# A second buffer for the transposed incidence, another order in the middle of each graph, and the output's scaling on GpSimd and ScalarE

## What is computed

```python
def hypergraph_conv(x, adj, W, b):
    H = (adj != 0).astype(x.dtype)
    w = adj.reshape(N, -1)[:, :C]
    xw = einsum('ncd,hd->nch', x, W)
    Dn = einsum('nce,ne->nc', H, w);  Dn = where(Dn > 0, 1/Dn, 0)
    Be = H.sum(axis=1);               Be = where(Be > 0, 1/Be, 0)
    m = Be[:, :, None] * einsum('nce,nch->neh', H, xw)
    return Dn[:, :, None] * einsum('nce,neh->nch', H, m) + b

def gnn(x):                       # 256 -> 512 -> 256
    h = layer_norm(relu(hypergraph_conv(x, adj, W1, b1)), gamma, beta)
    return hypergraph_conv(h, adj, W2, b2) + x

def ffn(x):
    topw, topi = top_k(x @ router_w + router_b, 2);  topw = softmax(topw)
    h = silu(einsum('td,edh->teh', x, expert_w) + expert_b)
    y = x + einsum('te,teh->th', mask(topi, topw), h) @ out_w + out_b
    return norm_w * (y / sqrt(mean(y * y) + 1e-6))

x = x + gnn(_layernorm(x))
x = x + ffn(_layernorm(x))
```

## Time and profile before

| what | us |
|---|---|
| median of 3 runs | 750.67 |
| lowest and highest | 749.53, 751.47 |
| the profiled execution, its time | 751.47 |
| the profiled execution, its span | 749.9 |
| TensorE busy | 705.3 |
| VectorE busy | 652.2 |
| ScalarE busy | 495.0 |
| GpSimd busy | 288.4 |

### The profile page before, as it was taken

How to read it: one execution, slowest core, us unless ns; L and a number is a source line. 1 busy time by engine, 2 the same in 40 slices (tenths; PEclk the granted TensorE clock), 3 DMA queues, 4 the chain that set the end, 5 groups by cost and what they waited for, 6 DMA issues and landing times.

```text
span 749.9 us, 16620 instructions
## 1 busy us (share of the span) xinstructions
PE 705.3 (94%) x5573; PEld 482.4 (64%) x5573; DVE 652.2 (87%) x1569; ACT 495.0 (66%) x971; POOL 288.4 (38%) x670
## 2 busy tenths in 40 slices
PE   4787999999999999999999999999999999999983
PEld 3364584766758486675858577584857768585671
DVE  4878888889898989989898899988899998988776
ACT  4655757667594856758585766858576685847562
POOL 4223334144353525444351434435153453524242
PEclk9988999999999999999999999999999999999997
DMA  8455538376583838657393765738385664727312
GB/s 290 169 110 201 113 89 239 67 225 131 162 178 94 240 64 229 135 172 164 90 245 60 237 122 182 154 105 231 62 247 111 202 134 129 184 64 184 58 29 56
DMA packets 42584, 111.65 MB, mean 149 GB/s; under 512 B 4160, under 2 KB 5312, under 8 KB 42560
## 3 DMA queue, kind: packets, MB, share of 16 engines
q0 software_dynamic: 13536, 41.42, 30.4%
q1 hardware_dynamic: 29024, 69.92, 28.3%
HBM read 69.91 MB, written 16.25 MB: 115 GB/s over the span
## 4 chain that ended last, share of the span: by engine, by line
DVE 29%; PE 26%; DMA 14%; ACT 13%; issue 12%; POOL 2%; SPq 2%; DVEq 0%; POOLq 0%; ACTq 0%
DMA xb<-xn 13%; PE bank L1261 5%; DVE comb L863 4%; PE bank L1263 4%; PE bank L1262 4%; PE bank L1346 4%; PE bank L1347 4%; DVE silu L859 4%; DVE hntl L878 3%; DVE z L867 3%; DVE ybn L980 2%; DVE x L974 2%; DVE h L741 2%; DVE ht L745 2%; ACT xsh L449 2%
## 5 line engine op out<-in xcount | busy, mean ns | idle before, releaser
L1261 PE MATMUL bank<-xth,ewh 128*128 128x512 f16 (+1 forms) x272 | 100.6, 370 | 2.1 <-DVE ewl L782 2.1
L1263 PE MATMUL bank<-xth,ewl 128*128 128x512 f16 (+1 forms) x272 | 100.7, 370 | 0.0
L1262 PE MATMUL bank<-xtl,ewh 128*128 128x512 f16 (+1 forms) x272 | 100.7, 370 | 0.0
L507 ACT ACTIVATE silu<-bank,ebcol,ksc 128x512 f32<-128x512 f32 x120 | 92.1, 769 | 7.3 <-PE bank L1263 7.2
L1261 PE MATMUL bank<-w2h,hnth 128*128 128x256 f16 x256 | 70.7, 276 | 3.3 <-DVE hntl L878 2.6
L1263 PE MATMUL bank<-w2h,hntl 128*128 128x256 f16 x256 | 70.5, 275 | 0.0
L1262 PE MATMUL bank<-w2l,hnth 128*128 128x256 f16 x256 | 70.5, 275 | 0.0
L548 ACT ACTIVATE a1h<-bank,be 128x256 f16<-128x256 f32 x64 | 26.8, 469 | 54.3 <-PE bank L1406 51.0
L654 ACT ACTIVATE uh<-bank,be 128x256 f16<-128x256 f32 x64 | 26.8, 470 | 53.4 <-PE bank L1347 53.4
L525 ACT ACTIVATE hnth<-bank 128x512 f16<-128x512 f32 x64 | 37.9, 592 | 33.3 <-PE bank L1315 33.3
L1405 PE MATMUL bank<-xsh,h 128*128 128x256 f16 x256 | 58.3, 277 | 0.9 <-DVE xsl L764 0.9
(11 more groups left out here) (248 smaller groups left out, 2138.3 us busy)
## 6 DMA issues: line engine op xcount, KB each, us to landing
adjin<-adj SPq DMA_DIRECT2D x16, 1024.0 KB, 5.3
adjtin<-adjt SPq DMA_DIRECT2D x16, 1024.0 KB, 6.2
xin<-x SPq DMA_DIRECT2D x16, 512.0 KB, 4.2
xb<-xn SPq DMA_DIRECT2D x16, 512.0 KB, 8.5
xb<-x POOLq DMA_DIRECT2D x16, 512.0 KB, 8.7
xb<-b POOLq DMA_DIRECT2D x16, 512.0 KB, 5.4
xb<-vadd POOLq DMA_DIRECT2D x16, 512.0 KB, 4.5
out<-x SPq DMA_DIRECT2D x15, 512.0 KB, 6.8
```

The costliest lines, as they stand in the source:

```text
L507: af(silu[:, i % 4, :], bank[E_BANK[i]][:, :], ACT.Silu, bias=ebcol[:, i:i + 1], scale=ksc[:, 2:3]).then_inc(silu_dn, 1)
L1261: mm(outp, lh, rh, start=first, stop=False)
L1262: mm(outp, lh, rl, start=False, stop=False)
L1263: return mm(outp, ll, rh, start=False, stop=last)
```

## The change

- **Two buffers.** `ht16` becomes a pair, one for even and one for odd graphs; the loop's body is written twice (six rounds of two graphs). `prep_ht(g)` moves from the start of body g to the end of body g - 1, between the first half of y and the remainder of U.
- **SyncE.** xb<-xn goes ahead of out<-x1 and of adjtin<-adjt, so it waits for x1 of graph f and for no incidence.
- **The output's scaling.** `finish` goes from VectorE's bodies (it stays in the tail). GpSimd multiplies y by the norm weights (`weigh_y`, two instructions of 128x512, ahead of `roots_y`), and ScalarE multiplies the result by the roots (`scale_y`, four of 128x256) as the first work of the next body. VectorE's `y_part(f, 0)` also waits until the y before has been weighed and squared.
- **The first sum of the experts** goes to GpSimd (`add_half`, 128x1024, behind the hidden tiles' roots). The last sum is split in two halves, and each half of the high part of `comb` waits for its own half.
- **ScalarE's middle.** Expert 1 and tanh stand ahead of `prep_x`; `mask_copy` stands ahead of `prep_x_hi`.
- **TensorE and VectorE.** The router's first two tiles wait for the first half of xtl alone; the last transposes of the hidden tile stand ahead of the second V tile; `hnt_part(g, 3)` stands ahead of the last sum, and `ct_part(f, 0)` ahead of `v_part(g, 0)`.

```diff
-        ht16 = sb("ht16", [P, CT, C], F16)
+        ht16 = (sb("ht16_even", [P, CT, C], F16), sb("ht16_odd", [P, CT, C], F16))
...
+            with eng.Fori(3, N - 2, 2) as g:
+                body(eng, g, 1, conv=True, ffn=True, late=True, prep=True)
+                body(eng, g + 1, 0, conv=True, ffn=True, late=True, prep=True)
...
+                if ffn:
+                    f = g - 1
+                    sp.wait_ge(x1_dn, 4 * f + 4)
+                if conv:
+                    if not prep:
+                        sp.wait_ge(xn_dn, 4 * g + 4)
+                    sp.dma_start(xb[:, :, :], xn[:, :, :]).then_inc(xn_kept, 16)
+                if ffn:
+                    sp.dma_start(out[f], x1[:, :, :]).then_inc(x1_st, 16)
+                if prep:
                     sp.wait_ge(ht_made, g + 1)
                     sp.dma_start(adjtin[:, :, :], adjt[g + 1].rearrange("(t p) c -> p t c", p=P)).then_inc(adjt_in, 16)
...
+            def weigh_y(f, j, again):
+                s = slice(CG * j, CG * j + CG)
+                gp.wait_ge(y_dn, 2 * f + j + 1)
+                if j == 0 and again:
+                    gp.wait_ge(out_st, 32 * f)
+                tt(yf[:, s, :], y[:, s, :], nwb[:, :].unsqueeze(1).to_broadcast([P, CG, D]), ALU.mult).then_inc(yw_dn, 1)
...
+            def add_half(f):
+                gp.wait_ge(comb_st, 7 * f + 2)
+                tt(comb[:, :, :], comb[:, :, :], silu[:, 2:4, :], ALU.add).then_inc(half_sum, 1)
...
+            def scale_y(act, q):
+                act.wait_ge(yw_dn, 2 * q + 2)
+                act.wait_ge(rr_st, 2 * q + 2)
+                for t in range(CT):
+                    af(yf[:, t, :], yf[:, t, :], ACT.Copy, scale=yrr[:, t:t + 1]).then_inc(yf_dn, 1)
...
             def combine_sum(f, e):
-                dve.wait_ge(comb_st, 7 * f + 2 * e)
-                TT(comb[:, :, :], comb[:, :, :], silu[:, 2 * (e % 2):2 * (e % 2) + 2, :], ALU.add).then_inc(comb_st, 1)
+                if e == 2:
+                    dve.wait_ge(half_sum, f + 1)
+                dve.wait_ge(comb_st, 7 * f + 2 * e - 1)
+                for s in ((slice(0, C),) if e == 2 else (slice(0, C // 2), slice(C // 2, C))):
+                    TT(comb[:, :, s], comb[:, :, s], silu[:, 2 * (e % 2):2 * (e % 2) + 2, s], ALU.add).then_inc(comb_st, 1)
...
                 if ffn and prep:
+                    if late:
+                        dve.wait_ge(yw_dn, 2 * f)
+                        dve.wait_ge(sq_dn, 4 * f)
                     y_part(f, 0)
+                if prep:
+                    prep_ht(g + 1, 1 - odd)
...
-                    pe.wait_ge(xt_lo, 2 * f + 2)
                     for t in range(CT):
+                        if t % CG == 0:
+                            pe.wait_ge(xt_lo, 2 * f + t // CG + 1)
```

More of the change, by code:

```diff
@@ L53, in build @@
     CG = 2
-    assert (C, D, DH, NE) == (512, 256, 512, 4)
+    assert (C, D, DH, NE) == (512, 256, 512, 4) and N % 2 == 0
     with ExitStack() as ctx:
@@ L221, in steps @@
         def steps(eng, body, tail):
[L223 to L228, removed]
+            body(eng, 0, 0, conv=True, ffn=False, late=False, prep=True)
+            body(eng, 1, 1, conv=True, ffn=True, late=False, prep=True)
+            body(eng, 2, 0, conv=True, ffn=True, late=True, prep=True)
+            with eng.Fori(3, N - 2, 2) as g:
+                body(eng, g, 1, conv=True, ffn=True, late=True, prep=True)
+                body(eng, g + 1, 0, conv=True, ffn=True, late=True, prep=True)
+            body(eng, N - 1, 1, conv=True, ffn=True, late=True, prep=False)
             tail(eng)
@@ L254, in _, with body @@
                 sp.dma_start(dst, src).then_inc(c_in, 16)
-            def body(sp, g, conv, ffn, late, prep):
+            def body(sp, g, odd, conv, ffn, late, prep):
                 if prep:
@@ L405, in body @@
                 if ffn and prep:
+                    weigh_y(f, 0, late)
+                    weigh_y(f, 1, late)
                     roots_y(f, ALL, 0)
@@ L556, in x2_part, with body @@
                        scale=yrs[:, t:t + 1]).then_inc(x2_dn, 1)
-            def body(act, g, conv, ffn, late, prep):
-                f = g - 1
+            def body(act, g, odd, conv, ffn, late, prep):
+                f, q = g - 1, g - 2
+                if late:
+                    scale_y(act, q)
                 if conv:
@@ L588, in body @@
                     expert(act, f, 0)
+                if ffn:
+                    expert(act, f, 1)
+                    act.wait_ge(arg_dn, f + 1)
+                    af(th[:, :, :], arg[:, :, :], ACT.Tanh).then_inc(th_dn, 1)
                 if prep and ffn:
                     prep_x(g + 1, (0, 1))
-                if ffn:
-                    act.wait_ge(arg_dn, f + 1)
-                    af(th[:, :, :], arg[:, :, :], ACT.Tanh).then_inc(th_dn, 1)
-                    expert(act, f, 1)
                 if prep and ffn:
@@ L992, in degrees, with body @@
                 v.reciprocal(be[:, :], dmax[:, :]).then_inc(be_dn, 1)
-            def body(dve, g, conv, ffn, late, prep):
+            def body(dve, g, odd, conv, ffn, late, prep):
                 f, q = g - 1, g - 2
@@ L1014, in body @@
                     a1_part(g, 0)
-                if late:
-                    finish(q, (0, 1), not ffn, not (isinstance(g, int) and g == 2))
                 if conv:
@@ L1020, in body @@
                     a1_part(g, 1)
-                if late:
-                    finish(q, (2, 3), not ffn, False)
                 if conv and not ffn:
@@ L1106, in body @@
                     hnt_part(g, 2)
+                if conv:
+                    hnt_part(g, 3)
                 if ffn:
@@ L1365, in turned_x2, with a2_half @@
                 ins.then_inc(xt_rdy, 1)
-            def a2_half(g, half, ffn):
+            def a2_half(g, odd, half, ffn):
                 pe.wait_ge(a1_lo, 4 * g + CG * half + CG)
@@ L1380, in a2_half, with body @@
                         ins.then_inc(a2_rdy, 1)
-            def body(pe, g, conv, ffn, late, prep):
+            def body(pe, g, odd, conv, ffn, late, prep):
                 f = g - 1
```

57 lines of the change are left out of this document (30 added, 27 removed).

## The result

| kernel | median us (lowest to highest) | runs |
|---|---|---|
| before, beside it | 750.9 (749.23 to 752.47) | 6 |
| changed | 745.98 (745.22 to 747.89) | 6 |

The ratio is 0.9942, 95% interval 0.9922 to 0.9962: faster by 0.6%, or 4.4 us by the ratio (the two medians are 4.9 apart). The profiled execution has a span of 744.6 us.

The account below looks back on a forecast made before the run. The prediction took TensorE, busy 94%, as the bound, with 0.87 us of waits in a mean body. Removing 13.6 us and adding 8.4 gave 5.2 less, a forecast of 746.0 us, with an 8-in-10 range of 737.0 to 752.5.

Parts of the forecast that it names:

- The waits of the kernel before: TensorE's waiting in a mean body of the kernel before: 0.22 + 0.32 + 0.33 = 0.87 us.
- three holes: TensorE waits before the router (xtl, 0.22 us), the mask's first row (mt, mean 0.32), the fourth V tile (hntl, 0.33).
- What the change takes away: TensorE's holes for xtl 3.3, mt 4.2, hntl 5.0 us, and body 1's degrees 1.1: together 13.6 us.
- a hole that moves on to ctl: Rival: a hole moves to the next late step, hntl or ctl, 0.3 us a body, 750; within the 0.22 case.
- The transfer: xb<-xn on SyncE is issued some 3 us earlier, ahead of the 1.5 MB of adjtin and out.
- ht in front of ul: Moved ht costs VectorE 1.2 us where it waited 1.25 for uh; costed at nothing, idle about 0.1 left.
- The first sum on GpSimd: 128x1024 sum, about 2.7 us, from near 522.6 to 525.3; cover 0.4 us before expert 6, cost taken as zero.
- The hole of x2: New TensorE wait before x2's transposes, released by ScalarE's x2: 0.6 us in bodies 2 to 15.
- The multiplication: GpSimd's second multiplication by the norm weights, held up by VectorE's h, ends about 1.2 us behind h's end.
- The price: Cost of moving the output's scaling: 14 bodies x 0.6 us = 8.4 us.
- The sum: Whole program: 13.6 - 8.4 = 5.2 us less; 745.5 for the median, rounded up to 746.0.
- The rival without a hole: GpSimd's multiplication is not held up by h, or only partly; all 13.6 us stay, 737.1; chance 0.15.

Follow-up runs that it names:

- the kernels without any wait: Changed kernel with scaling back on VectorE (738.24 us), with the sum back too (738.24), or with roots first, weights behind (739.29); period 42.48.
- the buffers alone: Kernel before plus ht16 pair, doubled loop, prep_ht behind y's first half and SyncE's new order: 742.28 us, ratio 0.9892.
- the order alone: Kernel before plus ScalarE's middle, router's half wait, earlier last hidden tile transposes and remainder; one buffer, old SyncE queue: 750.5 us, ratio 0.9988.
- in the other: Changed kernel with ScalarE multiplying y by the roots first, GpSimd by the weights behind, at the next body's start: 739.29 us, ratio 0.984.

## Why the prediction was right, point by point

- **The waits of the kernel before.** I had 0.87 us in a mean body; the kernels without any wait put it at 43.43 - 42.48 = 0.95 over eight bodies, and at 0.86 over the eleven from 192.90 to 669.63. The reading of three holes by the distances of starts holds.
- **What the change takes away: 13.6 us.** Measured with the scaling taken back: a ratio of 0.9833, some 12.5 us less, and 13.3 by the spans (749.9, 736.6). The term was a little too large. It also lies elsewhere in the program than I put it, by the starts of h in these two profiles. Bodies 0 and 1 gave 0.1 us together (104.24 and 104.11), where I had 1.1 for the degrees alone: the wait of 1.14 us for ht is gone, but in body 1 TensorE now waits 0.57 for x2 and 2.46 instead of 2.08 for the expert weights' remainder. Bodies 2 and 3 gave 3.7, where twice 0.87 was read. That the term came out near is in part luck. Its parts don't stand alone as I wrote them, each hole with an edit of its own: the buffers alone (with SyncE's order) shut two of the three holes, and the order alone shut nearly all and opened 0.64 us at ctl. I had named that case (a hole that moves on to ctl) for the changed kernel; it came in the half without the buffers.
- **The transfer.** xb<-xn is issued 3.78 us behind the start of h (496.19) where it was 7.22 (503.94), as I wrote, and lands in 4.1 us by the median where it took 8.5.
- **ht in front of ul.** VectorE's 1.25 us of idle went to none, not to 0.1 (489.68 follows ht at once), and no hole of TensorE in front of B3 came of it.
- **The first sum on GpSimd.** 2.36 us, not 2.7. The cover was spent even so: expert 6 waited 0.38 us for it, 4.8 us in 13 waits. I had misread the start. 522.6 is where the fourth root begins; its last step is the row below, of the kernel before. There it runs beside VectorE's own first sum (523.19 to 524.42); in the changed kernel it takes 0.19 us, and GpSimd's sum starts 0.14 behind its start. So the sum could start near 523.65 and end near 526.0, behind the 525.70 at which expert 6 was taken up:

```profile
523.51 0.96 POOL L324 TENSOR_TENSOR hnb<-hnm,hrs 128x1 f32<-128x1 f32 x1
```

The hole of x2 has no part in it: with the scaling taken back expert 6 waits as long, 5.0 us in 13 waits. As I wrote, it reached ScalarE and not TensorE: taken back, it changes nothing.

- **The multiplication.** Predicted to end 1.2 us behind h; it ended at 494.76, 1.13 behind 493.63. The roots: 1.30 predicted, 1.32 measured. Copies to a1h: 1.62 predicted, 1.61 measured. The hole: 0.6 predicted, 0.60 measured in this body and 0.63 in the mean. I hadn't seen that the first multiplication would be held up too, by ht; it ends before y's second half, and costs nothing.
- **The price.** 14 x 0.6 = 8.4 us predicted; 745.98 - 738.24 = 7.7 measured (on two chips), 8.0 by the spans.
- **The sum.** 5.2 us less by the terms, 4.4 measured by the ratio of 0.9942 and 4.9 by the medians, with 2.9 to 5.9 in the interval. The gains were 1.1 us too large and the cost 0.7, which nearly cancelled.
- **The rival without a hole** rested on the multiplication not being held up by h. It was held up. With h ahead of y it wasn't, and the hole was there, but then h itself stands ahead of y on the same path, so that kernel doesn't test the rival. The estimate above agrees with what I wrote there, that without the hold-up there would be no hole. What a run shows to remove it is that the multiplication leaves the front of the roots.

Open: how much of the 7 to 8 us by which the moved sum, the split and ctl's place help the kernel with one buffer and the new order belongs to which; which part of the buffers' gain is SyncE's order; and the changed kernel with the multiplication in front of the roots but not held up. That the block goes when the two engines touch other memory at the same moment wasn't tried.

## What to carry to other kernels

On an engine that is busy 94%, count the waits by the distance between starts; their sum was all that the changes to the other engines brought, here 0.95 us of a body, and the kernel is done when they are gone, whoever does the side work. When work moves to an engine with time to spare, look at what it is put in front of: GpSimd's 128x512 multiplication was dear by standing, under VectorE's h, in front of small roots for which ScalarE, and behind it TensorE, waits. And an edit that shuts a hole also takes away the time in which a third engine caught up: here the order alone gave 0.1%, and the order together with relief for VectorE 1.2% (the relief alone, in the old order, wasn't run).

## What the runs showed of the hardware

- A multiplication of 128x512 on GpSimd with a repeated row takes 1.27 us alone, 2.08 us when it starts 0.26 us behind the start of a 128x2048 comparison on VectorE, 2.19 us when it starts 0.16 us behind. It ends 1.12 and 1.13 us after the comparison, less than 1.27: a part of its time had passed while it was held up.
- It goes the other way too. A sum of 128x1024 on VectorE with both inputs in SBUF took 1.42 us instead of 1.22 when it started 0.34 us ahead of the end of such a multiplication, and a step of 128x1 on GpSimd that started under that sum took 1.18 us instead of 0.19.
- The Trainium skill ("Perfetto Trace Analysis", on optimizing Scalar and DVE operations) warns that moving work between GpSimd and VectorE might not help, as they share a port. Here it depended on the place: 8 us lost in one order, and in the other no more than 1 us (739.29 against 738.24, with overlapping intervals), with the same work on the same engines.
- A sum of 128x1024 in SBUF takes 2.36 us on GpSimd and 1.22 us on VectorE.
